# Layer norm sums: one product fewer for the mean and for the variance, and a second product in two pieces

## What is computed

```python
for i in range(DEPTH):                      # DEPTH = 6
    x = attn_layer(shift_tokens(x), Wqkv[i], q_scale[i], k_scale[i], Wo[i]) + x
    x = ffn_layer(shift_tokens(x), ln_g[i], ln_b[i], W1[i], b1[i], W2[i], b2[i]) + x

def ffn_layer(x, g, bln, W1, b1, W2, b2):
    mu = x.mean(-1, keepdims=True)
    var = ((x - mu) ** 2).mean(-1, keepdims=True)
    xn = (x - mu) / jnp.sqrt(var + 1e-05) * g + bln
    hg = xn @ W1 + b1
    a, gate = jnp.split(hg, 2, -1)
    return a * jax.nn.gelu(gate, approximate=False) @ W2 + b2
```

## Time and profile before

| | |
|---|---|
| median of 3 runs | 3271.54 us (3265.06 to 3272.32) |
| profiled execution, from its first to its last instruction | 3280.4 us |
| PE busy | 3087.2 us (94%) |
| DVE busy | 2638.4 us (80%) |
| ACT busy | 2534.1 us (77%) |
| POOL busy | 2084.0 us (64%) |
| granted TensorE clock, mean | 0.963 |

### The profile page before, as it was taken

The page is one execution under the profiler, slowest core; times in us unless marked ns, Lnnn a source line. Parts: engine busy times, 40 slices in busy tenths (PEclk is TensorE's granted clock), DMA queues, the critical chain, the costliest instruction groups (busy, mean ns, idle before and its releaser), DMA issues. The chain is left out here.

```text
span 3280.4 us, 80720 instructions
## 1 busy us (share of the span) xinstructions
PE 3087.2 (94%) x29936; PEld 2736.1 (83%) x29936; DVE 2638.4 (80%) x5117; ACT 2534.1 (77%) x7059; POOL 2084.0 (64%) x1536
## 2 busy tenths in 40 slices
PE   5898886689999999999999999999999999999997
PEld 4666664479998999989999989999899998999996
DVE  3378888878789888788878898878988878888884
ACT  2787885478787888788888888888788887888784
POOL 5347655776666666666666676667676767666661
PEclk8888996799999999999999999999999999999998
DMA  3111100110001000001100011000100000110000
GB/s 128 55 36 49 59 4 7 42 36 11 2 2 34 25 26 2 2 21 33 31 2 2 11 34 39 1 2 2 37 26 22 2 1 21 33 31 7 8 5 26
DMA packets 27780, 75.04 MB, mean 23 GB/s; under 512 B 4120, under 2 KB 9848, under 8 KB 27256
## 3 DMA queue, kind: packets, MB, share of 16 engines
q1 hardware_dynamic: 22224, 52.63, 5.1%
q0 software_dynamic: 4864, 16.78, 1.6%
q10 hardware_dynamic: 304, 0.47, 0.1%
HBM read 65.68 MB, written 4.19 MB: 21 GB/s over the span
## 5 line engine op out<-in xcount | busy, mean ns | idle before, releaser
L1596 POOL TENSOR_TENSOR turned<-by_cos,turned 128x512 f32<-128x512 f32 x384 | 494.5, 1288 | 827.5 <-DVE turned L2101 827.0
L1600 POOL TENSOR_TENSOR rnorm<-norm,half 128x8 f32<-128x8 f32 x384 | 789.1, 2055 | 0.0
L1883 ACT ACTIVATE prob<-ps_s,ebias,rnorm 128x128 f32<-128x128 f32 x1536 | 681.8, 457 | 64.9 <-DVE ebias L2122 64.2
L2115 DVE TENSOR_REDUCE negmax<-ps_s 128x8 f32<-128x1024 f32 x192 | 235.0, 1224 | 284.0 <-PE ps_s L1698 283.9
L1892 ACT ACTIVATE prob_t<-ps_t 128x512 f32<-128x512 f32 x384 | 230.3, 600 | 223.4 <-PE ps_t L1707 218.8
L2130 DVE TENSOR_TENSOR prob<-prob,rinv 128x512 f32<-128x512 f32 x384 | 375.8, 979 | 13.1
L1642 PE MATMUL ps_qk<-w_hi,x_hi 128*128 128x512 f32 x768 | 336.8, 438 | 18.8 <-DVE turned L2101 12.2
L1787 PE MATMUL ps_f<-hid_hi,w_hi 128*128 128x256 f32 (+1 forms) x1056 | 309.3, 293 | 5.7 <-DVE hid_lo L2176 5.6
L1883 ACT ACTIVATION_READ_ACCUMULATOR prob<-ps_s,ebias,rnorm 128x1 f32 x1536 | 311.1, 203 | 0.0
L1642 PE MATMUL ps_qk<-w_lo,x_hi 128*128 128x512 f32 x768 | 305.8, 398 | 0.0
L1642 PE MATMUL ps_qk<-w_hi,x_lo 128*128 128x512 f32 x768 | 305.7, 398 | 0.0
(11 more groups left out here) (289 smaller groups left out, 9779.6 us busy)
## 6 DMA issues: line engine op xcount, KB each, us to landing
w_raw<-in_w_qkv SPq DMA_DIRECT2D x24, 768.0 KB, 4.8
w_raw<-in_w SPq DMA_DIRECT2D x12, 693.0 KB, 4.0
w_raw<-in_w_o SPq DMA_DIRECT2D x12, 512.0 KB, 3.4
w_raw<-in_w SPq DMA_DIRECT2D x6, 768.0 KB, 4.4
x_tok<-in_x SPq DMA_DIRECT2D x8, 256.0 KB, 2.7
kept<-x_t SPq DMA_DIRECT2D x8, 256.0 KB, 2.0
w_raw<-kept SPq DMA_DIRECT2D x8, 256.0 KB, 3.1
out<-rows_out SPq DMA_DIRECT2D x8, 256.0 KB, 2.2
```

The costliest lines, as they stand in the source:

```text
L1596: G.tensor_tensor(turned[:, k, :], by_cos[:, :], turned[:, k, :], ALU.add).then_inc(s["turned"], 1)
L1600: G.tensor_tensor(rnorm[:, i % RR, :], norm2[:, k, :], half[:, :], ALU.pow).then_inc(s["rnorm"], 1)
L1883: last = A.activation(prob[:, k, h, :], half_bank(h % 2, k)[:, T(h // 2)], ACT.Exp, bias=ebias[:, i // NU % 2, k, h:h + 1], scale=rnorm[:, ...
L2115: V.tensor_reduce(negmax[:, k, :, :].rearrange("p u (c o) -> p o u c", o=2), ps_s[:, :, :].rearrange("p o (u c k) -> p o u c k", u=NU, c=2 ...
```

## The change

`add_x` gets a second instruction: DVE adds the two halves of `x1` into tile 2 of `hidden` (`halves`), and `mean_mm` multiplies that one tile, one product for two. The squares lie in tiles 3 and 4 of `hidden`; a new piece `add_squares` on DVE, behind `center`, adds them into tile 2 of `gate` (`squares`), and `var_mm` does two products for four. `square` on ACT no longer waits for POOL's `hid_lo` but for DVE's `gated`, and stands ahead of the unit's `project` in its step. `var_mm` moves to the front of its step on PE. `w_2_mm` for half 0 is cut: tiles 0 to 2 (9 products) go to step 8q+24, right behind the next pass's `mean_mm`, and tiles 3 to 5 (8 products) stay in step 8q+26.

```diff
-    cent, cent_sq = hidden[:, 0:KT, :], gate[:, 0:KT, :]
+    cent, cent_sq = hidden[:, 0:KT, :], hidden[:, 3:3 + KT, :]
+    halves, squares = hidden[:, KT, :], gate[:, KT, :]
 # PE
         def mean_mm(q):
-            E.wait_ge(s["lx1"], q + 1)
+            E.wait_ge(s["x1_and_halves"], 2 * q + 2)
...
-            for kt in range(KT):
-                last = E.matmul(ps_f[1][:, 0:N], mean_w[:, :], shifted(x1[:, q % 2, :])[:, kt, :], start=kt == 0, stop=kt == KT - 1)
-            last.then_inc(s["mean"], 1)
+            E.matmul(ps_f[1][:, 0:N], mean_w[:, :], halves, start=True, stop=True).then_inc(s["mean"], 1)
         def var_mm(q):
-            E.wait_ge(s["cent2"], q + 1)
+            E.wait_ge(s["cent_and_squares"], 2 * q + 2)
             for u in range(NU):
-                for kt in range(KT):
-                    last = E.matmul(ps_f[1][:, N + u:N + u + 1], cent_sq[:, kt, T(u)], mean_w[:, 0:1], start=kt == 0,
-                                    stop=kt == KT - 1)
+                last = E.matmul(ps_f[1][:, N + u:N + u + 1], squares[:, T(u)], mean_w[:, 0:1], start=True, stop=True)
...
+            for q in passes(t, 18):
+                var_mm(q)
             for q in passes(t, 26):
-                w_2_mm(q, 0)
+                w_2_mm(q, 0, range(3, NJ))
...
             for q in passes(t, 16):
                 mean_mm(q)
+            for q in passes(t, 24):
+                w_2_mm(q, 0, range(3))
 # ACT
         def square(q):
-            A.wait_ge(s["cent"], q + 1)
+            A.wait_ge(s["cent_and_squares"], 2 * q + 1)
             if q:
-                A.wait_ge(s["hid_lo"], 2 * q)
+                A.wait_ge(s["gated"], 2 * q)
 # DVE
         def add_x(q):
...
+            V.wait_ge(s["x1_and_halves"], 2 * q + 1)
+            if q:
+                V.wait_ge(s["gated"], 2 * q - 1)
+            by_half = shifted(x1[:, q % 2, :])
+            V.tensor_tensor(halves, by_half[:, 0, :], by_half[:, 1, :], ALU.add).then_inc(s["x1_and_halves"], 1)
+        def add_squares(q):
+            V.wait_ge(s["cent2"], q + 1)
+            if q:
+                V.wait_ge(s["hid_lo"], 2 * q - 1)
+            V.tensor_tensor(squares, cent_sq[:, 0, :], cent_sq[:, 1, :], ALU.add).then_inc(s["cent_and_squares"], 1)
...
             for q in passes(t, 17):
                 center(q)
+            for q in passes(t, 17):
+                add_squares(q)
```

More of the change, by code:

```diff
@@ L1420 @@
     "qk_square v_copied qk_t prob prob_t attn_hi cent2 lin_hi hid_read_act gelu hid_hi "
-    "qk_by_sin norm2 norm2_floor negmax ebias rinv prob_unit attn_lo lx1 cent spread normed lin lin_lo hid_read_dve gated "
+    "qk_by_sin norm2 norm2_floor negmax ebias rinv prob_unit attn_lo x1_and_halves cent_and_squares spread normed lin lin_lo hid_read_dve gated "
     "fed summed rnorm turned k_unit rstd hid_lo lset"
@@ L1789, in hidden_mm, with w_2_mm @@
             last.then_inc(s["hid"], 1)
-        def w_2_mm(q, mt):
+        def w_2_mm(q, mt, tiles):
             if q % B == 0:
                 E.wait_ge(s["low"], OTHER * (q // B + 1))
-            E.wait_ge(s["lx1"], min(q + 2, PASSES))
-            for j in range(NJ):
+            E.wait_ge(s["x1_and_halves"], 2 * min(q + 2, PASSES) - 1)
+            for j in tiles:
                 if j % 3 == 0:
@@ L1801, in w_2_mm @@
                                     x[:, j, :].bitcast(F32R), start=j + n == 0, stop=j == NJ - 1 and n == 1)
-            last.then_inc(s["out_ps"], 1)
+            if NJ - 1 in tiles:
+                last.then_inc(s["out_ps"], 1)
         E.wait_ge(s["lset"], 6)
@@ L1812, in pe @@
             for q in passes(t, 27):
-                w_2_mm(q, 1)
+                w_2_mm(q, 1, range(NJ))
             for i in units(t, 2):
@@ L1817, in pe @@
                 rstd_row_mm(q)
-            for q in passes(t, 18):
-                var_mm(q)
             for c in lates(t, 14):
@@ L1995, in act @@
                 head_mirror(c, 1)
+            for q in passes(t, 17):
+                square(q)
             for i in units(t, 0):
@@ L2007, in act @@
                 heads_out(c)
-            for q in passes(t, 17):
-                square(q)
             for c in lates(t, 13):
@@ L2144, in add_x @@
             V.tensor_tensor(whole(x1[:, q % 2, :]), ps_f[0][:, :].rearrange("p (k n) -> p k n", k=KT), whole(state[:, q % B, :]),
[L2145 removed]
+                            ALU.add).then_inc(s["x1_and_halves"], 1)
+            V.wait_ge(s["x1_and_halves"], 2 * q + 1)
[3 more added lines that the diff above has]
+            V.tensor_tensor(halves, by_half[:, 0, :], by_half[:, 1, :], ALU.add).then_inc(s["x1_and_halves"], 1)
         def center(q):
@@ L2152, in center @@
             V.tensor_tensor(cent[:, :, :], shifted(x1[:, q % 2, :]), ps_f[1][:, 0:N].unsqueeze(1).broadcast_to([P, KT, N]),
-                            ALU.subtract).then_inc(s["cent"], 1)
+                            ALU.subtract).then_inc(s["cent_and_squares"], 1)
+        def add_squares(q):
[3 more added lines that the diff above has]
+            V.tensor_tensor(squares, cent_sq[:, 0, :], cent_sq[:, 1, :], ALU.add).then_inc(s["cent_and_squares"], 1)
         def take_spread(q):
```

## The result

The changed kernel takes 3309.3 us (median of 4 runs, 3304.4 to 3316.1) beside 3271.1 for the kernel before (4 runs): ratio 1.0115, 95% interval 1.0096 to 1.0134. It is slower by 38 us. I had forecast 3278.5 with a range that ended at 3294.

The account below looks back on a forecast made before the run. PE bounds by busy time, but DVE's spare time of 1.02 us per pass was expected to decide. Regular passes -2.7, changes of layer +9.4, first and last passes +0.5: +7.2 us, forecast 3278.5, range 3255 to 3294.

Parts of the forecast that it names:

- DVE's spare time: Step 2, DVE's chain from negmax to prob before PE's flip_prob: 1.02 us spare per pass, expected to decide.
- PE's sum: PE's own saving from mean, variance and the vanished wait for ACT: 1.18 us per pass, 57 us in 48 passes.
- the mean: PE's mean group in step 0: 1.03 us, expected to halve, 0.51 us.
- The halves: DVE's sum ahead of prob in step 0: 0.41 us, prob still ahead of PE's request.
- The squares: DVE's add_squares held by POOL's hid_lo, about 1.9 us; negmax slips by 0.87 us.
- The step that failed: Step 2, negmax to flip_prob: 1.02 us spare less 0.87 slip leaves 0.15 us gain, 0.09 after rstd.
- Around a change of layer: Passes where DVE splits weights ahead of center: losses of 0.84, 0.5 and 0.53 us, five changes, +9.4 us.
- DVE wins the race: Rival: squares' sum comes before hid_lo in regular passes, POOL waits 0.35 us; -10.8 us, 3260.7; chance 13%.
- the sum runs beside: Rival: DVE's squares' sum runs beside POOL's hid_lo, changes of layer cost nothing; about -21 us, 3250.5; chance 10%.
- PE's sum counts in full: Rival: all of PE's saving shows, needing a DVE chain shorter than 4.75 us; -57 us, 3214.5; chance 5%.
- POOL becomes late for PE: Rival: rstd and the keys' scaling in step 3 pushed 0.3 us further; 14.4 us on top, 3293; chance 10%.
- the rival of the held halves: Rival: rnorm holds the halves' sum in step 0, PE 1.15 us late every pass; +55 us, 3327; chance 3%.

Follow-up runs that it names:

- the reduction: Changed kernel with the squares summed by a one-input tensor_reduce instead of the two-input tensor_tensor: 3273.4 us, ratio 0.9996 to the kernel before.
- eight products behind the projection: Changed kernel with the 8 remaining products of half 0 moved from ahead of the projection to behind it: 3386.6 us, ratio 1.0340 to the kernel before.
- squares only: Changed kernel without the halves' sum, second product whole in step 2, variance behind the transpose, square at its new place: 3290.8 us, ratio 1.0053.
- halves only: Changed kernel without the squares' sum, variance again by four products, square and variance at their new places, three tiles moved: 3258.1 us, ratio 0.9956.
- tiles moved back: Changed kernel with half 0 of the second product whole again in step 2: 3319.5 us, ratio 1.0132 to the kernel before.
- halves, two tiles: Changed kernel without the squares' sum and with two tiles (6 products) moved instead of three; the fastest of all: 3253.0 us, ratio 0.9931.
- sum behind the maxima: Changed kernel with the two-input squares' sum behind the row maxima and ebias on DVE, variance products at their old place: 3272.4 us, ratio 0.9994.

## Why the prediction was wrong

**What bounds.** That DVE's spare time decides and not PE's sum was right, and so was the size of the slip: `negmax` 0.88 us later, forecast 0.87. DVE's busy time rose by 113 us (2638.4 to 2751.5), forecast 110. On PE's side the mean was a little over-priced, at 0.51 us for 0.43: half of the group's 1.03 us counts half of its last instruction's end, which overlaps what follows. The scores came 0.16 us later (5.47 us after the mean instead of 5.31), forecast 0.33. Neither mattered, since PE's sum did not decide.

**The halves.** Forecast 0.41 us, measured 0.43, held by nothing. With its tiles and the new places, and without the squares' sum, the edit gains 0.4 to 0.7%. The prediction put this gain at the size that was left over by the squares and never by itself.

**The squares.** Forecast 1.93 us and held until `hid_lo` is over; measured 1.95. The race that could have gone the other way did not happen, the sum never came first in a regular pass, and the reduction shows that the hold is the cause.

**The step that failed** is "From the start of `negmax` to the end of `prob` are 4.75 us. PE asks 1.07 us later". That treats the stretch from the scores to `flip_prob` as if PE met DVE only at its end. It meets it sooner: the projection writes `ps_qk`, of which there is one, and has to wait until `turned` has read it. In the kernel before, `turned` ended at 1745.81 and the projection came at 1746.60; less the 0.15 us that lie between the two where PE does wait, the spare time there was 0.64 us. The same slip of 0.87 then gives 0.23 us of loss per regular pass, and not 0.15 of gain. Measured: 0.27. The eight products behind the projection show the meeting directly, and the squares only show it with no tile moved. So do all the kernels side by side, here in one regular pass (number 19), in us from the start of its mean:

| kernel | `turned` ends | projection starts | pass |
|---|---|---|---|
| before | 9.24 | 10.03 | 53.99 |
| changed | 10.12 | 10.27 | 54.31 |
| halves only | 9.40 | 9.55 | 53.49 |
| squares only | 9.96 | 10.10 | 54.07 |
| squares' sum as a reduction | 9.41 | 9.55 | 53.51 |
| tiles moved back | 10.11 | 10.32 | 54.27 |
| halves, two tiles | 9.25 | 9.39 | 53.33 |
| sum behind the maxima | 9.71 | 9.86 | 53.80 |
| eight products behind | 10.12 | 10.26 | 55.18 |

But for the kernel before and the one with the tiles back, the projection follows `turned` by 0.14 or 0.15 us. And from the projection on, the pass takes 43.9 to 44.0 us in all but the last, which has eight products more there.

The row was in the trace of before, among the waits: `PE ps_qk L1642 <- DVE turned L2101: 0.9, 5, 0.2`. All five lie in the passes 6, where `turned` is late. They do not measure the reserve of a regular pass, but they name the place where PE meets DVE ahead of `flip_prob`.

This error is 0.36 us per pass (-0.09 to +0.27), about 11 us over the 30 passes that the prediction called regular.

**Around a change of layer** the forecast was +9.4 us; the passes 6, 7 and 0 together cost 21.4. There I had followed `negmax` to `prob`, and not to `turned`. The squares only, where PE never waits at the variance, lose 18.1 us in the same passes (8.0, 3.9 and 6.2), with longer waits for `turned` and no other new wait above 0.2 us. In the changed kernel PE stands at the variance first, which I had forecast at 0.4 us for a regular pass: up to 2.28 us in a pass 6, 1.10 in a 7 and 0.98 in a 0, as `square` and the sum follow a weight split. Much of that is, I take it, time that it would else have waited at the projection; no run separates the two.

Behind the wait of the pass 6 comes the fall of the clock, on which the prediction has no word. What a fall costs can be read from passes 6 of one kernel that differ in nothing else. In the halves only three of the five beside a change of layer have it and are 0.7 us longer than before, two have not and are 0.2 to 0.3 shorter; with the sum behind the maxima it is 1.1 and 1.2 us longer against 0.0 to 0.1. So a fall costs 1.0 to 1.1 us there, and the six of the changed kernel make 6 to 7 of its 32 us, by this estimate.

The pass 5, which I counted as regular, costs 0.75: PE waits 0.52 us for `prob` there, since DVE's halves and the splits come before it. The halves only and the fastest kernel show the same 0.52 and yet come out even there, or 0.2 us below.

**The rivals.** "DVE wins the race" and "the sum runs beside" did not occur. "PE's sum counts in full" did not either. Among those that made it slower, "POOL becomes late for PE" had the right size per pass, 0.3 us, and the wrong engine: PE does not wait for POOL in the regular passes. The 1737.26 for `prob` in the rival of the held halves does not follow from its rows, which give 1736.44 + 0.69 = 1737.13; that rival did not occur either.

**What is not settled:** the layers' +32 us leave 3 to 6 us of the 35 to 38 between the medians. The part ahead of them scatters by more than that, so I can't say whether they belong to the change.

## What to carry to other kernels

Before you spend a chain's spare time, walk down the whole chain and note every place where the other engine meets it, buffers that are written anew included; the reserve is the smallest of them, not the last. When an addition on VectorE falls under a long GpSimd operation, try a form with one SBUF input or another place in the list, even if it is longer by itself: here 0.70 us beat 0.43. And take a change apart, since one part of this one, the halves' sum with two tiles moved and the new places, is a gain of 0.7% that the squares' sum hid.

## What the runs showed of the hardware

- A two-input sum of 128x256 on VectorE takes 0.43 us by itself and up to 1.95 when GpSimd's 128x768 operation has just begun; a one-input reduction over the same data takes 0.69 to 0.72 us beside that operation.
- The time that is added is the rest of GpSimd's operation less 0.15 us. In the trace of before, 331 instructions `prob` (two inputs, 0.69 us by themselves) start under POOL's 128x512 `turned`, with more than 0.15 us of it left, and take 0.98 to 1.22 us, each to within 0.02 us what this gives. POOL's 128x8 `rnorm` does not hold them: 47 start under it and take 0.69.
- After some waits of PE the granted clock fell, with all the rest at 2.4 GHz. In the passes 6 of the changed kernel it fell after waits of 2.25 to 2.28 us, each time; in the eight products behind, after waits of 0.33 and 1.74 us shortly after each other, in 9 passes of 24. The length of the wait does not decide alone: with the sum behind the maxima it fell in two passes 6 of five after 2.05 to 2.09 us, and in the halves only in three of five after 0.98. After waits of 0.32 and 0.75 us per pass it never fell. A fall made a pass 1.0 to 1.6 us longer, and the busy share alone does not show it; the clock by slices does.
